# Attention on one core: the product with v taken for two neighbouring heads at a time

## What is computed

```python
q = einsum('bsh,he->bse', x, w_q).reshape(b, sq, GROUPS, HPG, KVC)      # 16 heads of 128, 4 groups
k, v = split(einsum('bsh,he->bse', x, w_kv), 2)                          # k and v of 4 groups
scores = einsum('bqgpd,bkgd->bgqpk', q, k) * SCALE
scores = where(causal, scores, -inf)
probs = softmax(scores, axis=-1)
ctx = einsum('bgqpk,bkgd->bqgpd', probs, v).reshape(b, sq, HEADS * KVC)
return einsum('bse,eh->bsh', ctx, w_dense)                               # added to x
```

## Time and profile before

| | |
|---|---|
| median of 3 runs | 2638.76 us (2637.43 to 2639.93) |
| profiled execution | 2639.36 us, span 2637.5 us |
| PE busy | 2536.8 us, 96% of the span |
| DVE busy | 2157.0 us, 82% |
| ACT busy | 946.0 us, 36% |
| POOL busy | 910.4 us, 35% |
| TensorE clock granted, mean | 0.989 |

### The profile page before, as it was taken

The page is one execution under the profiler, slowest core; times in us unless marked ns, Lnnn a source line. Parts: engine busy times, 40 slices in busy tenths (PEclk is TensorE's granted clock), DMA queues, the critical chain, the costliest instruction groups (busy, mean ns, idle before and its releaser), DMA issues. The chain is left out here.

```text
span 2637.5 us, 45987 instructions
## 1 busy us (share of the span) xinstructions
PE 2536.8 (96%) x14500; PEld 2341.1 (89%) x14500; DVE 2157.0 (82%) x6164; ACT 946.0 (36%) x2546; POOL 910.4 (35%) x1952
## 2 busy tenths in 40 slices
PE   6999999999996999999999999997999999999998
PEld 6999999999995889898888988896899999999997
DVE  6888888888886788888888888886888888888887
ACT  3111101111113677777777777774211011111100
POOL 4332333233224334343434343333423333332321
PEclk9999999999998999999999999998999999999999
DMA  6000000000001454554455455555100000000000
GB/s 192 9 1 1 1 1 1 1 1 1 1 27 56 81 91 91 89 89 84 91 91 88 83 93 88 89 90 121 51 1 9 9 1 9 9 9 1 9 9 9
DMA packets 378738, 117.30 MB, mean 44 GB/s; under 512 B 338560, under 2 KB 377472, under 8 KB 378496
## 3 DMA queue, kind: packets, MB, share of 16 engines
q1 hardware_dynamic: 378496, 114.36, 22.1%
HBM read 26.24 MB, written 4.19 MB: 12 GB/s over the span
## 5 line engine op out<-in xcount | busy, mean ns | idle before, releaser
L555 PE MATMUL ffn_ring<-ffn_mix_weights,ffn_yT 128*128 128x384 f32 x5760 | 1154.9, 341 | 8.1 <-DVE ffn_mix_weights L790 5.8
L555 PEld LDWEIGHTS ffn_ring<-ffn_mix_weights,ffn_yT 128*128 128x128 f32 x5760 | 1007.1, 189 | 58.5 <-DVE ffn_mix_sums L725 15.7
L727 DVE SCALAR_TENSOR_TENSOR ffn_mix_sums<-ffn_ring,ffn_w,ffn_mix_sums 128x384 f32<-128x384 f32 x896 | 550.4, 615 | 241.5 <-PE ffn_ring L555 224.8
L1579 POOL CAST attn_probsT<-attn_turned 128x1024 fp32r<-128x1024 f16 (+3 forms) x512 | 348.5, 723 | 508.1 <-DVE attn_probs L1444 496.9
L605 PE MATMUL ffn_ring<-ffn_out_weights,ffn_avT 128*128 128x512 f32 x1536 | 440.4, 397 | 7.0 <-POOL ffn_avT L1028 4.5
L1512 ACT ACTIVATE attn_exponentials<-attn_exponentials,attn_score_neg_max 128x512 f32<-128x512 f32 (+3 forms) x512 | 285.6, 558 | 169.8 <-DVE attn_score_neg_max L1427 169.6
L605 PEld LDWEIGHTS ffn_ring<-ffn_out_weights,ffn_avT 128*128 128x128 f32 x1536 | 281.2, 188 | 36.2 <-POOL ffn_avT L1028 5.7
L1273 PE MATMUL attn_ctx<-attn_probsT,attn_v 128*128 128x256 f32 (+2 forms) x1536 | 276.1, 329 | 14.9 <-issue 7.8
L1273 PEld LDWEIGHTS attn_ctx<-attn_probsT,attn_v 128*128 128x128 f32 x1536 | 242.1, 190 | 37.3 <-issue 9.3
L1444 DVE SCALAR_TENSOR_TENSOR attn_probs<-attn_exponentials,attn_prob_factor,attn_probs 128x512 f16<-128x512 f32 (+3 forms) x512 | 254.3, 558 | 22.0 <-ACT attn_probs L1521 21.3
L1521 ACT ACTIVATE attn_probs<-attn_exponentials,attn_prob_factor 128x512 f16<-128x512 f32 (+3 forms) x512 | 250.1, 552 | 27.5 <-DVE attn_prob_factor L1437 16.0
(11 more groups left out here) (141 smaller groups left out, 2858.8 us busy)
## 6 DMA issues: line engine op xcount, KB each, us to landing
ffn_mix_stage<-in_L_ffn_q_proj_dram SPq DMA_DIRECT2D x32, 128.0 KB, 2.5
ffn_mix_stage<-in_L_ffn_k_proj_dram SPq DMA_DIRECT2D x32, 128.0 KB, 2.5
ffn_mix_stage<-in_L_ffn_v_proj_dram SPq DMA_DIRECT2D x32, 128.0 KB, 2.9
ffn_out_stage<-in_L_ffn_o_proj_dram SPq DMA_DIRECT2D x16, 256.0 KB, 3.0
attn_turned<-attn_probs SPq DMA_TRANSPOSE x256, 4.0
out_dram<-x SPq DMA_DIRECT2D x8, 512.0 KB, 2.9
x<-in_L_attn_x_dram SPq DMA_DIRECT2D x7, 512.0 KB, 8.1
early_stage<-in_L_attn_w_q_dram SPq DMA_DIRECT2D x4, 512.0 KB, 5.3
```

What stands on the lines that cost most here:

```text
L555: last = pe.matmul(bank[:, 0:QKV], yT[:, t % 2, h, k * P:(k + 1) * P], mix_half(e, wh)[:, k], start=(n == 0), stop=(n == 3 * CK - 1))
L727: dve.scalar_tensor_tensor(into, bank[:, 0:QKV], w[:, t, e:e + 1], into, ALU.mult, ALU.add).then_inc(mix_done, 1)
L1579: pool.tensor_copy(cast(i), landed(n, i).rearrange("p (j h q) -> p j h q", h=HL, q=P)).then_inc(t_cast, 1)
```

## The change

Two neighbouring heads of a group (even h and h+1) share one product with v. In an even slot PE takes the *long* rows, row tiles 3 and 2 of both heads, with all four key blocks: widths 512, 512, 512, 256. In the odd slot it takes the *short* rows, tiles 1 and 0 of both, with two key blocks: widths 512 and 256. No block of zeros is left. The transposed probabilities stand in two tensors, `pT_long` and `pT_short`, at steps of four blocks, and the turned float16 blocks in `turned_long` (2 buffers) and `turned_short` (3). Since both heads of a pair must be there first, the product comes one slot later (`LAST_LAG` 4 for 3), and so do `dense` and `add_to_x`; the casts of the short rows move from lag 2 to lag 3. `dense` now takes one half of the rows of two heads instead of two halves of one head, again 12 matmuls in two steps. `add_to_x` of the two halves stands in slots 2 and 3 instead of both in slot 2. `cT` has one buffer for two; in the last four slots every second context uses a projection bank and `zT`. `z` takes the place of the first group of `kT`, which makes room.

```diff
-PT_STEP = 3 * P
-PT_COLS = 13 * P
-LAST_LAG = 3
+PAIR_STEP = 4 * P
+LONG_COLS = 14 * P
+SHORT_COLS = 6 * P
+LAST_LAG = 4
...
-            blocks = pT[:].rearrange("p h (b q) -> p b h q", q=P)
-            return blocks[:, i:i + 3 * i + 1:3]
+            blocks = (pT_long if pair_of(i) else pT_short)[:].rearrange("p h (b q) -> p b h q", q=P)
+            first = n % 2 + (0 if i % 2 else 2)
+            return blocks[:, first:first + 4 * i + 1:4]
...
-                    reach(sp, t_cast, done_of(n - 2, 2 * pair))
+                    if pair:
+                        reach(sp, long_cast, 2 * (n - 1))
+                    else:
+                        reach(sp, short_cast, 2 * (n - 2))
...
             def attend(u):
                 b, h, n = u
-                pe.wait_ge(t_cast, QT * n + QT)
+                long = h % 2 == 0
+                pe.wait_ge(long_cast if long else short_cast, 2 * (n // 2 * 2 + 2))
...
-                for j in range(QT):
-                    q0 = min(j, 2)
-                    at = j * PT_STEP + q0 * P
-                    mm = product(cx[:, q0 * P:SEQ], lambda a: v[:, j, a, g * D:(g + 1) * D],
-                                 lambda c: pT[:, c, at:at + SEQ - q0 * P], j == 0, j == QT - 1)
+                buffer, blocks = (pT_long, QT) if long else (pT_short, 2)
+                for j in range(blocks):
+                    width = 4 * P if j < blocks - 1 else 2 * P
+                    mm = product(ctx_bank(n)[:, 0:width], lambda a: v[:, j, a, g * D:(g + 1) * D],
+                                 lambda c: buffer[:, c, j * PAIR_STEP:j * PAIR_STEP + width], j == 0, j == blocks - 1)
...
-            def dense(u, half):
+            def dense(u, member):
                 b, h, n = u
-                if half == 0:
+                half, first = 1 - h % 2, h // 2 * 2
+                if member == 0:
                     pe.wait_ge(c_lo, n + 1)
...
+                for t in range(2):
+                    at = (member + (0 if t else 2)) * P
+                    row = (first + member) * C
...
+                if h == LAST_LAG - 2 and last and b < B or h == LAST_LAG - 1 and b == B:
+                    add_to_x(b - 1, 1)
                 if h == LAST_LAG - 1 and last:
-                    add_to_x(b - 1)
+                    add_to_x(b - 1, 0)
...
-                reach(pool, c_ready, n)
+                reach(pool, c_ready, n // 2 * 2 - 1 if pair_of(i) else n // 2 * 2)
...
-                    for half in range(HL):
-                        at = 3 * PT_STEP + 2 * P
-                        pool.memset(as_f32(pT[:, half, at:at + P]), 0.0).then_inc(zeroed, 1)
-                u = unit(b, h, 2)
-                if u:
-                    if u[2] + 1 < B * HEADS:
-                        pool.wait_ge(p_lo, done_of(u[2] + 1, 0))
-                    for i in reversed(range(QT)):
-                        cast_turned(u, i)
+                long, short = unit(b, h, 2), unit(b, h, 3)
+                if long and long[2] + 1 < B * HEADS:
+                    pool.wait_ge(p_lo, done_of(long[2] + 1, 0))
+                if short and h % 2 == 0:
+                    cast_turned(short, 1)
+                    cast_turned(short, 0)
+                if long:
+                    cast_turned(long, 3)
+                    cast_turned(long, 2)
+                if short and h % 2:
+                    cast_turned(short, 1)
+                    cast_turned(short, 0)
```

More of the change, by code:

```diff
@@ L1159, in sem @@
             return ctx.enter_context(nc.semaphore(f"attn_{n}"))
-        kT = nc.alloc_sbuf_tensor_at("attn_kT", [P, GROUPS, HL, SEQ], F32R, offset=nc.sbuf_base)
+        kT_at = nc.sbuf_base
+        kT = nc.alloc_sbuf_tensor_at("attn_kT", [P, GROUPS, HL, SEQ], F32R, offset=kT_at)
         sb("early_space", [P, aw.words()])
@@ L1195, in attention @@
         p_hi, p_lo = sem("prob_hi"), sem("prob_lo")
-        t_landed, t_cast = [sem(f"turned{i}") for i in range(QT // 2)], sem("probsT")
+        t_landed = [sem(f"turned{i}") for i in range(QT // 2)]
+        long_cast, short_cast = sem("long_probsT"), sem("short_probsT")
         c_ready, c_hi, c_lo = sem("c_ready"), sem("c_hi"), sem("c_lo")
@@ L1342, in dense @@
                     pe.wait_ge(aw.lo_pool, EARLY - 2 + LATE)
[L1343 to L1349, removed]
+                if first == 0 and member == 0:
+                    reach(pe, x_added, 2 * b - half)
+                for t in range(2):
+                    at = (member + (0 if t else 2)) * P
+                    row = (first + member) * C
+                    mm = product(dn[half][:, t * C:(t + 1) * C], lambda a: ctx_half(n, a)[:, at:at + P],
+                                 lambda c: wd[:, c, 0, row:row + C], first + member == 0 and t == 0,
+                                 first + member == HEADS - 1)
+                if first + member == HEADS - 1:
                     mm.then_inc(d_ready, 1)
@@ L1450, in split_context, with add_to_x @@
                 dve.wait_ge(c_hi, n + 1)
-                dve.scalar_tensor_tensor(cT[:, h % 2, 1], cx[:], 1.0 / PROB_SCALE, as_f32(cT[:, h % 2, 0]),
+                dve.scalar_tensor_tensor(ctx_half(n, 1), ctx_bank(n)[:], 1.0 / PROB_SCALE, as_f32(ctx_half(n, 0)),
                                          ALU.mult, ALU.subtract).then_inc(c_lo, 1)
[L1454 to L1458, removed]
-                    dve.tensor_tensor(x, x, dn[half][:], ALU.add).then_inc(x_added, 1)
+            def add_to_x(b, half):
+                dve.wait_ge(d_ready, 2 * b + 2 - half)
+                x = m.x[:, b * QT + 2 * half:b * QT + 2 * half + 2, :].rearrange("p t c -> p (t c)")
+                dve.tensor_tensor(x, x, dn[half][:], ALU.add).then_inc(x_added, 1)
             def slot(b, h):
@@ L1526, in split_context @@
                 act.wait_ge(c_ready, n + 1)
-                act.activation(cT[:, h % 2, 0], cx[:], ACT.Copy, scale=1.0 / PROB_SCALE).then_inc(c_hi, 1)
+                act.activation(ctx_half(n, 0), ctx_bank(n)[:], ACT.Copy, scale=1.0 / PROB_SCALE).then_inc(c_hi, 1)
             def slot(b, h):
```

44 lines of the change are left out of this document (27 added, 17 removed).

## The result

The changed kernel takes 2625.08 us (median of 6 runs, 2623.55 to 2628.32); beside it the kernel before took 2638.79 (6 runs, 2637.43 to 2640.27). The ratio is 0.9949, with a 95% interval of 0.9938 to 0.9960: 0.5% faster. The profiled execution has a span of 2623.1 us, 14.4 less than before.

A forecast was written before the change was run, and what follows sets the result against it. PE was taken to bound slots 0 to 8, a DVE/ACT loop slots 9 to 15. Savings of 9.8 (seven items), 0.4 (item 7), 3.6 (start), 1.4 (end), 15.2 us in all, gave 2623.5; 8-in-10 range 2612 to 2634.

The forecast's parts named there:

- The bound and its split: PE bounds slots 0 to 8 of an item; a loop of DVE and ACT steps, period about 6.65 us, bounds the rest.
- M0 to M9: From row tile 3's score maximum in slot 0 to that in slot 9: 68.17 us before, forecast near 66.8.
- M9 to M0: From tile 3's maximum in slot 9 to that in the next item's slot 0: 51.66 us before, forecast 51.7.
- The product: Product with v on PE: long 2.46, short 1.05 us; a pair costs 3.51 for 3.86, columns deciding.
- Slots 0 to 8: Long slots +2.65, short -3.52, slot 2's wait -1.14, new waits in slots 3 and 5 +0.61: -1.4 us an item.
- -1.14 for slot 2: PE's 1.14 us wait for the last v's split at the end of slot 2 goes, as head 0 comes later.
- Slots 9 to 15: The DVE and ACT loop sets the pace: nothing lost or won; PE's wait in slot 15 grows from 0.69 to 1.5.
- The start and the end: Item 0 without a product in slot 3: -3.6 us; shorter tail after the last casts: -1.4 us.
- these transfers at no cost: SP's transfers wait behind POOL's long casts, which finish in time: no cost to ACT.
- The loop gives nothing back: Rival: the loop sets short slots' periods, so they save nothing; an item +0.9 us, 2639, no change; chance 0.12.
- The clock falls: Rival: PE's longer wait in slot 15 drops the clock; 3.5 us an item would give 2651; chance 0.07.
- More is kept: Rival: no waits in slots 3 and 5, PE's savings show in slots 9 to 15 too; 2614; chance 0.11.

The follow-up runs named there:

- experiment 1: Changed kernel with three 256-column matmuls added to each short product, restoring the columns of before: 2631.79 us, ratio 0.9966.
- experiment 6: Changed kernel with the low half of the context behind the maximum of tile 2 on DVE, in even slots: 2620.90 us, ratio 0.9933.
- experiment 2: Kernel before, with the last two v projections of the first half issued one place earlier: 2633.09 us, ratio 0.9976.
- experiment 3: Changed kernel with the last two v projections of the first half issued one place earlier: 2625.32 us, ratio 0.9945.
- experiment 5: Changed kernel with the second half of a long product's `dense` moved to the start of the odd slot: 2617.12 us, second measurement 2618.14.
- the unedited run: Changed kernel measured again without edits, beside some of the follow-up kernels: 2622.58 us, ratio 0.9936.
- experiment 7: Changed kernel with half of `dense` moved and the low half of the context later on DVE: in all slots 2620.25 us, in even slots only 2614.25.
- experiment 4: Changed kernel with the v projections of place E moved from long slots 2, 4, 6, 8 into short slots 1, 3, 7, 9: 2625.62 us.
- the fastest kernel: Changed kernel with half of `dense` moved to the odd slot and the low half of the context later in even slots only: 2614.25 us.

## Why the prediction was right

**The bound and its split.** M0 to M9 moved and M9 to M0 did not, as forecast; experiments 1 and 6 show it from two sides: work for PE costs in the one part and hardly in the other, order on DVE gains in the other.

**The product.** 2.46 and 1.05 us were forecast, 2.43 and 1.05 measured. Seen from start to start, columns alone set it.

**Slots 0 to 8.** The waits in slots 3 and 5 were put at 0.36 and 0.25 and are 0.39 and 0.24. M0 to M9 was put at 66.8; it is 66.8 to 67.3 in items 1 to 6 and 66.1 in item 7. The term was -1.4 an item and came out as -1.3 (9.3 / 7). Its two parts held too: fewer columns 2.65 - 3.52 = -0.87, measured 0.75 less in experiment 1; waits and the later slot -1.14 + 0.61 = -0.53, measured 0.57 less. But that PE is the bound in every one of these slots did not hold, and the sum hides it. M0 to M1, where a short product of 0.88 us less comes in, got 0.15 longer (6.69 to 6.84 in the mean of items 1 to 6), since before it already stood at the loop's own period; M4 to M9 of item 0, with two long and three short products, did not move at all. Most of the term, 0.9 of 1.3, was won by M4. But its part of -1.14 for slot 2 is shown only in part: experiment 2, which takes that wait away alone, got 0.72. That the change got all of it, since its slot 3 has no product that needs the new v, follows from its trace (no idle time before the short product at 981.27) and from experiment 3, not from a run that isolates it.

**Slots 9 to 15.** PE's wait in slot 15 was put at 1.5 and is 1.52. That a long slot with `dense`, product and scores behind the maximum (6.26 us) stays under the loop held.

**The start and the end** were each put too small by half a microsecond. At the start the product was taken as warm, which was the good end of the range, and it was: 2.46 us, with the clock at 0.77 from 862 to 870, up from 0.51. Which end comes is partly luck: of the two measurements of experiment 5, one kernel, the first had a clock of 0.84 there and 36.65 us from M0 to M4, the second 0.67 and 37.41; experiment 3 had 0.50 and 38.50. At the end the forecast had a first short product of 1.9 us, cold, and it took 1.16 (1792.64 to 1793.80); the long one was taken as warm at 2.46 and took 3.15. These two errors cancel. The half microsecond is that the short product began 8.36 us behind the maximum of slot 15 (1784.28 to 1792.64), where the forecast had 8.96. Item 7 gained 1.0 for 0.4, and all of it between M9 and M10 (7.73 us before, 6.65 after). The stretches behind M10 stood still, where the forecast counted on slots 10 and 11.

**What the sum did not hold.** The 2.2 us in M9 to M0 come nearly all from item 3 (last section): ACT waited there for transposed probabilities. The forecast had moved these transfers at no cost, as long as POOL's casts don't hold them up. They don't: SP waits 0.6 us in all for the long casts between 920 and 1810 us. Yet they land late, and ACT waits 16.2 us for them in all, for 10.2 before. This term was put at nothing, and 2.1 us were lost in one item. That the change brings this loss is not shown: experiment 1 has the same transfers and does not have it. The -1.0 and +0.8 stand in the two expert blocks, which the change does not touch. Without these three the span would have been 16.4 us shorter, so the sum of 15.2 was 1.2 too small, and that it comes within 0.8 of the 14.4 measured is in part that such errors cancel. The 1.6 us between forecast and time are less than the 2.5 between two measurements of the same kernel, and tell nothing of a term.

**The rivals.** "The loop gives nothing back" fell with M0 to M9 and with experiment 1. "The clock falls" fell as a cost in each item: the granted clock is 1.00 in both parts of an item, with a wait of 1.5 us in slot 15 of each. But the sign that the prediction named for it, a clock that leaves 1.00 inside an item, did come once, in item 3 of the unedited run, at a cost of 1.2 us (last section). The Trainium skill's account of a clock that goes back and forth between short groups of matmuls ("TensorE: Matmul & The Clock Gate", "A second HAM failure mode") has no counterpart inside the items, with that one fall in eight of them; the kernels of experiments 5 and 7 have 8 and 14 us less of these waits (14.1 and 8.4 for 22.5) and a mean clock of 0.990 and 0.987, for 0.988 in after. "More is kept" did not happen in the changed kernel: M9 to M0 stood still.

## What to carry to other kernels

Cut a period into the part where one engine has no gaps and the part where it waits for a loop of other engines, and count savings of that engine only in the first; in the second, the order of the loop's own steps is what there is to gain. When two work items share an operation, look at what the pair's uneven halves do to each slot: the saving came with two new waits of 0.6 us an item. Moving half of `dense`, which brings nothing for the other engines and stood in front of a v that DVE waits for, got 0.8 us an item; moving the v projections themselves to other slots got nothing in the whole. And put the old amount of work back once: here it showed that more than half of the gain came with the later slot and not from the smaller product. A wait that a longer lag removes can often be had by issuing its cause one place earlier.

## What the runs showed of the hardware

A transposing transfer can land late and hold ACT, which may not overwrite the probabilities before. In the kernel after this happened twice in item 3, behind M10 and behind M13. The first time in ACT's timeline:

```profile
1278.96 1.92 ACT L1550 ACTIVATE attn_probs<-attn_exponentials,attn_prob_factor 128x512 f16<-128x512 f32 x4 [1.55 <-DMA attn_turned_long<-attn_probs]
```

The transfer was issued at 1273.00, so ACT went on 6.0 us later; the median from issue to landing of such a transfer is 4.0 us. The second wait is 1.33 us, at 1301.12. M10 to M11 is 8.03 us for 7.02 before, M13 to M14 7.96 for 6.83. M9 to M0 of item 3 is 53.95 us there, 55.18 in the unedited run, 53.2 to 54.3 in experiments 3 to 6 and in the fastest kernel, 52.4 with the context later in all slots, but 51.8 before and 51.9 in experiments 1 and 2; most other items stay near 51.7. So it comes back in the same stretch of most kernels and is missing in others. What delays the transfer wasn't settled.

In the unedited run PE stood 1.76 us for the maximum there, and then the clock fell inside the item (the wait, and the stretch around it with columns as in rows 1):

```profile
1281.68 0.38 PE L1333 MATMUL attn_scores<-attn_kT,attn_qT 128*128 128x256 f32 x1 [1.76 <-DVE attn_score_neg_max L1456]
...
1280.00:1290.00 10.00, 8.32 (x38) 7.32 (x39) 8.29 (x27) 6.70 (x17) 4.62 (x9) 0.83 0.41 78
```

The profiled execution of after, the same kernel, has a wait of 1.75 us at the same place and stays at 1.00. M11 to M12 is 7.70 us in it and 8.89 in the unedited run.

The first product of the block ran at full speed after a stretch with 0.46 us of idle time in 8, where before, with 1.56 idle, it took nearly double. The idle time of that stretch does not decide it: in experiment 3 PE was idle 0.58 us of the 8 and the clock was 0.50, in the second measurement of experiment 5 it was not idle at all and the clock was 0.67. At the end of the block the clock fell behind a wait of 2.94 us, while waits of 1.5 us in each item left it at 1.00 (in the first measurement of experiment 5 it fell behind the wait of 1.46 us in slot 15 of item 7, to 0.66 from 1780 to 1784). The stretch behind that wait, in the kernel after (columns as in rows 1):

```profile
1793.80:1799.40 5.60, 5.60 (x27) 4.99 (x26) 0.69 (x1) 0.60 (x1) 4.12 (x7) 0.70 0.08 15
```

PE is without a gap there, and the first product behind the wait still ran at full speed (1.16 us); the fall shows in the two groups after it, `dense` 2.36 us for 1.4 and the long product 3.15 for 2.43. So it comes late, and goes while PE works.
